# A decoder layer on one core: the PSUM banks of the attention front go from four to two, and one transpose moves to another bank

## The reference

```
x  = layernorm(x + attention(x))          # 16 heads, three branches
x  = layernorm(x + cross(x, context))     # 16 heads of 16
x  = layernorm(x + experts(x))            # 8 experts, 256 -> 1024 -> 256, weighted sum of all

attention: nq = rms(x @ w_cq);  q = nq @ [w_dq_nope | w_dq_rope], rope on the last 64
           ckv = rms(x @ w_ckv); k1, v1 from ckv, rope part shared      -> causal
           64 tokens by top_k(x @ w_imp); ks, vs from x[those]          -> not causal
           kw, vw = x @ w_wink, x @ w_winv                              -> causal
           gate = softmax(mean(x @ w_gate)); out = (g0 a1 + g1 a2 + g2 a3) @ w_proj
```

## Time and profile before

| | |
|---|---|
| median of 3 runs | 1725.67 us (1725.42 to 1726.9) |
| the profiled execution | 1726.9 us, its span 1724.9 us |
| mean granted PE clock | 0.988 of full speed |
| attention and cross, rows 0 to 7 | to about 900 us |
| experts | about 900 us to the end |
| distance from one woven front to the next | 116.8 us (118.13, 234.98, 351.57, 468.36, 584.93, 701.53 us; the seventh woven front begins at 820.07) |

### The profile page before, as it was taken

The page is one execution under the profiler, slowest core; times in us unless marked ns, Lnnn a source line. Parts: engine busy times, 40 slices in busy tenths (PEclk is TensorE's granted clock), DMA queues, the critical chain, the costliest instruction groups (busy, mean ns, idle before and its releaser), DMA issues.

```text
span 1724.9 us, 33531 instructions
## 1 busy us (share of the span) xinstructions
PE 1654.1 (96%) x11320; PEld 1350.0 (78%) x11320; DVE 1156.8 (67%) x3826; ACT 845.0 (49%) x2760; POOL 1038.3 (60%) x1451
## 2 busy tenths in 40 slices
PE   6799999999999999999999799999999999999998
PEld 5577676776776767767766479999999999999997
DVE  4567767877777687777776577566656665657557
ACT  1475857947848668579487632222222222222221
POOL 2465756746747657458476586565656565657553
PEclk9799999999999999999999989999999999999999
DMA  7202103012021030120120010101010101010001
GB/s 217 64 2 72 29 13 88 2 43 58 2 60 41 1 91 11 30 71 2 45 49 30 23 50 25 50 1 50 1 49 1 50 1 49 1 50 1 1 1 49
DMA packets 52458, 63.52 MB, mean 37 GB/s; under 512 B 12288, under 2 KB 40448, under 8 KB 52160
## 3 DMA queue, kind: packets, MB, share of 16 engines
q1 hardware_dynamic: 52288, 61.38, 12.6%
HBM read 29.89 MB, written 2.10 MB: 19 GB/s over the span
## 4 chain that ended last, share of the span: by engine, by line
PE 79%; ACT 6%; DVE 5%; issue 4%; POOL 3%; SPq 2%; DMA 0%; DVEq 0%; POOLq 0%; ACTq 0%
PE ps_Y L2226 20%; PE ps_H L2226 19%; PE ps_S L1440 19%; PE ps_O L1440 5%; ACT pr L884 5%; PE ps_T L1661 5%; PE ps_X L1440 4%; PE ps_T L1440 2%; POOL pr L726 2%; SPq L578 1%; PE ps_T L1779 1%; PE ps_S L1779 1%; DVE sm L1351 1%; DVE h_hi L2189 1%; POOL rot L672 1%
## 5 line engine op out<-in xcount | busy, mean ns | idle before, releaser
L2014 POOL TENSOR_TENSOR h_lo<-h_sb,h_hi 128x512 fp32r<-128x512 f32 x256 | 363.7, 1449 | 108.6 <-DVE h_hi L2189 108.6
L2060 ACT ACTIVATE h_sb<-ps_H,b_sb 128x512 f32<-128x512 f32 x256 | 176.7, 690 | 508.3 <-PE ps_H L2226 481.9
L691 POOL TENSOR_TENSOR pr<-pr,rden 128x128 f32<-128x128 f32 (+2 forms) x768 | 308.0, 437 | 108.2 <-DVE rden L1232 108.0
L2189 DVE CAST h_hi<-h_sb 128x512 fp32r<-128x512 f32 x256 | 239.0, 951 | 130.7 <-ACT h_sb L2060 130.6
L884 ACT ACTIVATE pr<-sm,nmx 128x128 f32<-128x128 f32 (+2 forms) x768 | 311.6, 412 | 29.9 <-DVE nmx L1243 29.8
L2226 PE MATMUL ps_Y<-w_hi,h_lo 128*128 128x256 f32 x1024 | 286.5, 280 | 0.0
L2226 PE MATMUL ps_Y<-w_hi,h_hi 128*128 128x256 f32 x1024 | 286.5, 280 | 0.0
L2226 PE MATMUL ps_Y<-w_lo,h_hi 128*128 128x256 f32 x1024 | 286.4, 280 | 0.0
L1243 DVE CUSTOM_DVE_ANT_0 sm<-ps_S,cmask 128x128 f32<-128x128 f32 (+2 forms) x768 | 192.8, 308 | 46.8 <-PE ps_S L1440 34.8
L726 POOL TENSOR_TENSOR pr<-pr,rden 128x256 f32<-128x256 f32 x256 | 151.0, 615 | 109.4 <-DVE rden L1232 109.4
L2226 PE MATMUL ps_H<-x_hi,w_hi 128*128 128x512 f32 x512 | 200.8, 392 | 0.0
(11 more groups left out here) (257 smaller groups left out, 3148.2 us busy)
## 6 DMA issues: line engine op xcount, KB each, us to landing
qT_sb<-rot SPq DMA_DIRECT2D x256, 64.0 KB, 2.0
w_raw<-in_W SPq DMA_DIRECT2D x16, 1024.0 KB, 6.2
kT_sb<-rot SPq DMA_DIRECT2D x192, 64.0 KB, 2.0
xin<-in_x SPq DMA_DIRECT2D x8, 256.0 KB, 2.8
cin<-in_ctx SPq DMA_DIRECT2D x8, 256.0 KB, 2.6
w_kw<-in_wink SPq DMA_DIRECT2D x2, 768.0 KB, 7.1
w_ks<-in_selk SPq DMA_DIRECT2D x2, 768.0 KB, 10.3
out<-x SPq DMA_DIRECT2D x3, 512.0 KB, 3.0
```

The lines of the kernel that those rows point to most:

```text
L691: last = pool.tensor_tensor(p_, p_, rden[:, h % 2, n:n + 1].to_broadcast([P, width]), ALU.mult)
L2014: pool.tensor_tensor(h_lo[:, s % 2, ht, :], h_sb[:, ht % 4, :], h_hi[:, s % 2, ht, :].bitcast(F32), ALU.subtract).then_inc(lo_sb.sem, 1)
L2060: ins = act.activation(h_sb[:, ht % 4, :], pst[plan.bank(f)][:, :], ACT.Relu, bias=b1[:, 2 * i + s // NCH, ht:ht + 1])
L2189: dve.tensor_copy(h_hi[:, s % 2, ht, :], h_sb[:, ht % 4, :]).then_inc(hi_sb.sem, 1)
```

## The change

The list of front fills goes round two banks, S2 and S3, where it went round four (S2, S3, X, T1). `latT` leaves the list and goes to T1, ahead of the two `ksT`, which keep X and T1. The steps of the engines, the instructions and the transfers stay as they are; what changes is on which bank a fill lies, and so which earlier fill PE waits for before it.

```diff
-FRONT_BANKS = ("S2", "S3", "X", "T1")
 ...
     for n, name in enumerate((
             "first", "imp", ("kw", 0, "a"), ("kw", 0, "b"), ("kw", 0, "n"), "gate",
-            ("kw", 1, "a"), ("kw", 1, "b"), ("kw", 1, "n"), ("vw", 0), "latT", ("vw", 1),
+            ("kw", 1, "a"), ("kw", 1, "b"), ("kw", 1, "n"), ("vw", 0), ("vw", 1),
             ("q", 0, "a"), ("q", 0, "b"), ("q", 0, "n"), ("q", 0, "c"),
             ("q", 1, "a"), ("q", 1, "b"), ("q", 1, "n"), ("q", 1, "c"),
             "pos", ("v1", 0), "xsel", ("v1", 1), ("ks", "ab"), ("ks", "nv"))):
-        plan.add(name, FRONT_BANKS[n % len(FRONT_BANKS)], ahead=True)
-    for n, name in enumerate((("ksT", 0), ("ksT", 1))):
-        plan.add(name, ("X", "T1")[n % 2], ahead=True)
+        plan.add(name, f"S{2 + n % 2}", ahead=True)
+    for n, name in enumerate(("latT", ("ksT", 0), ("ksT", 1))):
+        plan.add(name, ("T1", "X")[n % 2], ahead=True)
```

## The result

The change makes the kernel slower: 1739.22 us median of seven runs (1733.08 to 1741.3), beside 1726.9 us for the kernel before in the same session. The ratio is 1.006, with a 95% interval of 1.0046 to 1.0075, so 8 to 13 us. The forecast was 1733.4 us, that is 7.7 us more than the 1725.67 us that the kernel before took in its first three runs. All 24 runs of after on record lie between 1732.87 and 1741.32 us, with a median of 1737.6. The profiled execution of after took 1735.02 us, its span is 1733.0 us.

A forecast was written before the change was run, and what follows sets the result against it. PE, busy 96% of the span, was taken to bound the kernel. Seven woven fronts at 1.1 us each gave 7.7 us, all other terms 0, so 1725.67 + 7.7 = 1733.4 us; range 1729 to 1739.5.

The forecast's parts named there:

- Removed part, kw fills, `latT`: 0.: Woven fronts: dropping waits behind X and T1 gains 0; kw fills and `latT` on T1 cost 0.
- Steps 1 and 2: Woven front: `q 0 b` waits for ACT's read of `vw 1`; it and `q 0 n` start 0.28 us late.
- Step 3: Woven front: `q 1 a` waits for ACT's late copy of `q 0 n`, starting 1.07 us late.
- Step 4: Woven front: the `scores_x` after the first two q 1 fills starts 0.75 us late.
- Step 5: Turned probabilities: the 0.61 us pause for POOL takes lateness to 0; `values_x`, waiting for ACT, is 0.28 us late.
- Step 6: `q 1 n` and `q 1 c` wait for DVE's late rope products: 0.93 and 1.16 us late; next `scores_x` 1.07.
- Not given back: Rest of woven front: PE feeds the other engines, so pauses stay and all 1.1 us per front counts.
- Row 0: 0: Row 0's front: some 3.0 us of lateness hides under 3.4 us of cover from SP's transfers, costing 0.
- soaked up: Woven fronts' 2.4 us of pauses absorb the lateness, leaving 0.28 us each, 1727.7 us; chance 16%.
- more waits: PE also held at other zero-distance fills, one more stall per front, about 6 us on top, 1739.7 us; chance 22%.
- faster: New pauses bring PE and its suppliers into better order, winning 9.1 us, 1716.6 us; chance 5%.
- The clock rival: Woven fronts: more frequent pauses drop PE to 1.2 GHz from the first new stall, over 200 us; chance 2%.

The follow-up runs named there:

- the first experiment: Changed kernel with the eight q fills alone spread back over four banks, all other fills on two; 1730.12 us, ratio 1.0006.
- second: Kernel before with only the q fills (and `pos`, `v1 0`) on two banks, the others on four; 1735.79 us, ratio 1.0052.
- ninth experiment: Changed kernel with `q 0 b` alone moved to X; 1739.47 us, ratio 1.0060.
- the fifth: Changed kernel with ACT's copies of `q 0 n` and `q 0 c` one front step earlier, same banks; 1731.16 us, ratio 1.0016.
- the sixth experiment: Changed kernel with the even cross heads' turned probabilities on X instead of S0; 1736.18 us, ratio 1.0047.
- the fourth experiment: Changed kernel with `q 1 n` on X and `q 1 c` on T1, so neither waits for DVE; 1732.71 us, ratio 1.0033.
- the eighth experiment: Changed kernel run again unchanged in another session against the kernel before; 1739.27 us, ratio 1.0064.
- probabilities on X with three banks: Changed kernel with even cross heads' turned probabilities on X, q fills and what follows on S2, S3, T1; 1728.01 us, ratio 1.0003.
- whole list on three: Changed kernel with the whole fill list going round S2, S3 and X, `latT` on T1; 1727.69 us, ratio 0.9999.

## Why the prediction was right, and which terms were off

The direction, the place and the engines were right. The price per front is 1.38 us instead of 1.1: 9.7 instead of 7.7 us, inside the 8 to 13 of the ratio. The time falls in the range, but only just: 1739.22 against an upper end of 1739.5. Of the 5.8 us above the forecast 2.0 are the fronts' higher price, 1.2 are that the kernel before had a median of 1726.9 and not 1725.67 over seven runs, and 2.6 are not explained. That the sum stayed in the range is in part luck.

- **Removed part, kw fills, `latT`: 0.** Right for the woven fronts, by the first experiment (1.0006; no bank wait at those fills in its fronts). In row 0 the kw fills do stall, 0.33 and 0.40 us, which the prediction had named as a sign of being wrong; it costs nothing there, because head 0 waits for SP.
- **Steps 1 and 2**, 0.28 us: 0.23 and 0.32, the second with the longer first product behind the stall. They cost nothing by themselves (second and ninth experiment).
- **Step 3**, 1.07: 1.02. The hand-over was 0.06 us and not 0.1. That ACT's place behind its exponentials sets it is shown by the fifth.
- **Step 4**, 0.75: 0.89. The mis-sized term is the time of the two q 1 fills after the stall. I took 8 x 0.216 = 1.73 us; from 394.67 to 396.59 it was 1.92. Of the 0.19 too few, 0.10 is the first product behind the stall, which takes longer (1.99 instead of 1.89 for the eight; 402.93 - 401.87 = 1.06 instead of 398.46 - 397.50 = 0.96 behind `q 1 c`). The other 0.09 could have been read before: eight q products with `scores_x` right behind them took 386.85 - 385.03 = 1.82 us.

```profile
386.85 1.13 PE L1440 MATMUL ps_S<-kx_sb,qx_sb 32*128 32x256 f32 x8
```

- **Step 5 failed.** It held that the 0.61 us pause before the probabilities on S0 takes the lateness in, because POOL was named as its releaser. Measured: 0.79 late. That fill also needs S0 read by DVE, and in before DVE had done so only 0.2 us before POOL was done:

```profile
394.24 0.42 DVE L1351 CUSTOM_DVE_ANT_0 sm<-ps_S,sm 128x256 f32<-128x256 f32 x1
```

  It ends at 394.66, POOL at about 394.87. DVE's read is fed by the late `scores_x`, so it moved with the lateness: in after it ends at 398.66, 0.92 us later counted from the front's start, and PE goes at 398.82, while POOL had ended at 396.77 + 1.19 = 397.96. In the waits view that is the line that went from 7 to 14 times. The forecast's total survived this error because step 6 went through DVE, which bypasses PE's pause; the sixth experiment shows that this path sets `q 1 n` alone. Where that path is cut, as in the fourth experiment, the error shows at its full size.
- **Step 6**, 0.93, 1.16 and 1.07: 1.07, 1.29 and 1.39, step 4's 0.14 carried on, and the second longer fill.
- **Not given back**: right. 1.39 at `scores_x` is 1.43 at head 0 and 1.38 at the next front, and `ksT` waits 2.9 us in all in both kernels.
- **Row 0: 0**: right by head 0's start. At most 3.0 us of lateness were forecast, and at `pos` it was 2.48. It was gone before the end of the front: the products of `ks` began at 52.55 instead of 53.54, since in before PE had waited 1.18 us for DVE between them and `pos` and was at the lower clock there (below). So `ksT` was copied at 60.92, and the 3.4 us of cover were not put to the test.
- **The signs.** The distance was forecast 1.1 us longer and was 1.38. The pauses came where they were forecast and behind the readers that were named, but shorter: 0.53 instead of 0.8 before `q 1 a`, 0.23 instead of 0.6 before `q 1 n`, and one too short to be listed instead of 0.3 before `q 1 c`. At `q 1 n` the reason is step 5: PE was already 0.76 us late at `values_x`. PE's busy time did not stay, it rose by 0.78 us per front.
- **Rivals**: soaked up fell with the equal distances, more waits fell with the kw fills of the woven fronts at their old places (its price was also a slip: 1.28 - 0.49 is 0.79 us, not 0.9), faster fell with seven fronts all longer. The clock rival asked for some 33 us at 1.2 GHz in each front behind the new stalls; the clock keeps 1.00 there in all but one of 28 fronts (below).

The Trainium skill ("Perfetto Trace Analysis", section "Matmuls") says that independent groups of matmuls should go round different PSUM banks, so that reading one overlaps the next. The runs agree, and show how many banks it takes here: the ratio is 1.006 on two and 0.9999 on three.

What stays open: the medians differ by 12.3 us and the fronts explain 9.7. The interval of the ratio covers both. With all 24 runs of after the difference is 10.7, and in the session of the eighth experiment it is 1739.27 - 1728.9 = 10.4, so most of the remainder looks like the spread of seven runs. Whether any is left beside the chance of where clock drops fall was not tested.

## What to carry to other kernels

When two fills share a bank, look at the readers' place in their queues, not at how long they read: here a 0.56 us copy behind another job's exponentials cost 0.7 us a front. A pause swallows lateness only if none of its conditions hangs on the late work; the releaser that the trace names is the last of them, so look up when each of the others was met. Lateness travels by more than one path, here on PE itself and through DVE, which PE feeds; take each path alone, since the later one decides.

## What the runs showed that I had not expected

**The clock drops for a moment at other places in each execution.** Runs of one kernel spread by several us (after from 1732.87 to 1741.32), and these drops are the main difference that the profiles of one kernel show. In the profile of after, a window in the stretch that starts head 0 of row 4:

```profile
541.80:545.00 3.20, 3.20 (x11) 2.52 (x11) 0.95 (x8) 0.76 (x5) 0.87 (x2) 0.50 0.00 0
```

A granted clock of 0.50 is the lower level, 1.2 GHz, and PE was busy throughout. That front is 119.65 us long instead of 117.98. Before it PE had paused 0.51, 0.65 and 0.40 us within some 5 us, around the turning of `ksT`. Over the 12 profiles (84 woven fronts) 18 such drops lie in woven fronts, and 15 of them at this place, 67.3 to 69.1 us into the front; the other three, at 52 to 53 us, have no pause over 0.3 us in the 8 us before them. It happens in before as well (one front of 118.54), and a drop makes its front 1.4 to 1.7 us longer, the one of double length 3.3. Every front has pauses at head 0, and 69 of the 84 have no drop there.

The new stalls don't add drops. In the 28 fronts that have them both as in after (after, after again, only q on two, `q 0 b` apart) there are six drops at head 0 and one at 53.1 us, 7 us behind the second stall. In the 28 fronts of the kernels that have neither (before, q on four, probabilities on X with three banks, whole list on three) there are six at head 0 and one at 51.8 us. The Trainium skill ("TensorE: Matmul & The Clock Gate", section "A second HAM failure mode: psum-queue depth-cycling") ties such swings to small pauses between groups of matmuls. The place of the 15 agrees with it, the new stalls do not, and no run here varied the pauses at head 0.

**The last part moves too.** From the seventh front on, after took 904.31 us and before 904.78, though the front in it is 1.4 us longer; the second profile of after took 909.29. So one execution's span is no measure of a change of 0.5%, while the distances of undisturbed fronts repeat to 0.1 us.

**Row 0's clock.** The nine products of `ks` that took 2.36 us in after took twice as long in before:

```profile
53.54 4.53 PE L1440 MATMUL ps_S<-w_ks,lat 128*64 128x512 f32 x9
```

The window from 46 to 68 us has a clock of 0.83 where it was 0.64: in after the clock stayed at 2.4 GHz until 60.4 us, in before it had fallen to 1.2 GHz at 48.7. Head 0 did not gain by it, since it waits for SP's 20.56 us of transfers. Whether PE's later start on `pos`, which left it no pause of 1.18 us, is why the clock held was not tested.
